# Three changes to an audio tower on one core: who subtracts attention's low parts, fp32 products in the mixture, and where attention's buffers begin

## The reference, cut to what matters

```
h = conv tower(x)
h = h + attention(norm(h))      # 32 query heads, 8 key/value heads, rope, head size 128
h = h + mixture(norm(h))        # top-1 of 8 experts, rank 16
h = h + delay average(norm(h))  # autocorrelation, top 6 lags
h = h + routed linear(norm(h))  # 1024 x 1024 and 8 low-rank experts
```

```
q, k, v = x @ Wq.T, x @ Wk.T, x @ Wv.T          # Wq 4096 x 1024, Wk and Wv 1024 x 1024
out = softmax(rope(q) rope(k).T / sqrt(128)) v  # 4 query heads per key/value head
attention = out @ Wo.T                          # Wo 1024 x 4096

logits = x @ route_w.T                          # 8 experts
weight = one_hot(argmax(logits)) * max(logits)
mixture = (weight * (x @ A.T)) @ Bw.T           # A: 8 x 16 rows, Bw: 8 x 16 columns
```

## Time and profile before

| | us |
|---|---|
| median of 3 runs | 3120.15 (3115.19 to 3120.90) |
| the profiled execution's own time | 3115.31 |
| its span, first to last instruction | 3113.6 |
| attention, from its first projection to its last add | 311.15 to 2513.6 |
| mixture, to its last add | 2513.6 to 2636.6 |

### The profile page before, as it was taken

How to read it: one execution, slowest core, us unless ns; L and a number is a source line. 1 busy time by engine, 2 the same in 40 slices (tenths; PEclk the granted TensorE clock), 3 DMA queues, 4 the chain that set the end, 5 groups by cost and what they waited for, 6 DMA issues and landing times. The chain is left out here.

```text
span 3113.6 us, 37983 instructions
## 1 busy us (share of the span) xinstructions
PE 2854.7 (92%) x13353; PEld 2308.7 (74%) x13353; DVE 1594.4 (51%) x2914; ACT 982.6 (32%) x2029; POOL 915.5 (29%) x394
## 2 busy tenths in 40 slices
PE   8993999999899999989999998999999878749999
PEld 6762777777777777777777777777777667538888
DVE  4886544455544445555444455544445457563222
ACT  3553323333332223333222333232233223531111
POOL 2110433344333334433333442333334100241010
PEclk9995999999999999999999999999999978879999
DMA  5320322223222222322222232222223111010000
GB/s 114 69 54 9 102 75 74 74 88 93 63 75 75 74 74 88 91 65 76 75 74 74 81 93 63 82 75 74 74 71 91 34 55 41 1 61 28 28 27 28
DMA packets 55613, 207.20 MB, mean 67 GB/s; under 512 B 6928, under 2 KB 7312, under 8 KB 53456
## 3 DMA queue, kind: packets, MB, share of 16 engines
q1 hardware_dynamic: 55504, 205.79, 22.2%
HBM read 197.37 MB, written 8.39 MB: 66 GB/s over the span
## 5 line engine op out<-in xcount | busy, mean ns | idle before, releaser
L728 POOL TENSOR_TENSOR at_wlo<-at_wstage,at_whi 128x1024 fp32r<-128x1024 f32 x192 | 477.7, 2488 | 1437.0 <-ACT at_whi L751 1437.0
L993 PE MATMUL at_proj<-qr_xhi,at_whi 128*128 128x512 f32 x1536 | 635.1, 413 | 53.4 <-POOL at_wlo L728 49.0
L995 PE MATMUL at_proj<-qr_xhi,at_wlo 128*128 128x512 f32 x1536 | 609.3, 397 | 0.0
L994 PE MATMUL at_proj<-qr_xlo,at_whi 128*128 128x512 f32 x1536 | 608.8, 396 | 0.0
L993 PEld LDWEIGHTS at_proj<-qr_xhi,at_whi 128*128 128x128 f32 x1536 | 290.2, 189 | 131.2 <-issue 52.7
L994 PEld LDWEIGHTS at_proj<-qr_xlo,at_whi 128*128 128x128 f32 x1536 | 290.3, 189 | 69.9 <-issue 7.5
L995 PEld LDWEIGHTS at_proj<-qr_xhi,at_wlo 128*128 128x128 f32 x1536 | 289.5, 188 | 70.5
L1041 PE MATMUL at_out<-at_wohi,at_ohi 128*128 128x512 f32 x1008 | 314.3, 393 | 8.2 <-DVE at_wolo L720 6.2
L720 POOL TENSOR_TENSOR at_wolo<-at_ostage,at_wohi 128x1024 fp32r<-128x1024 f32 x126 | 312.0, 2497 | 32.7 <-ACT at_wohi L757 32.7
L1041 PE MATMUL at_out<-at_wolo,at_ohi 128*128 128x512 f32 x1008 | 312.5, 391 | 0.0
L1041 PE MATMUL at_out<-at_wohi,at_olo 128*128 128x512 f32 x1008 | 312.5, 391 | 0.0
(11 more groups left out here) (253 smaller groups left out, 4537.1 us busy)
## 6 DMA issues: line engine op xcount, KB each, us to landing
at_wstage<-in_w_qkv_dram SPq DMA_DIRECT2D x192, 512.0 KB, 3.6
at_ostage<-in_w_o_dram SPq DMA_DIRECT2D x128, 512.0 KB, 3.8
cv_x<-in_x_dram SPq DMA_DIRECT2D x32, 512.0 KB, 6.6
out_dram<-h SPq DMA_DIRECT2D x16, 512.0 KB, 2.7
fn_w_lo_raw<-in_w_t_dram SPq DMA_DIRECT2D x8, 512.0 KB, 6.6
fn_qka_lo_raw<-in_qka_t_dram SPq DMA_DIRECT2D x5, 512.0 KB, 5.4
sc_fhi_raw<-in_dft_fwd_dram SPq DMA_DIRECT2D x4, 512.0 KB, 7.1
sc_chi_raw<-in_lag_cos_dram SPq DMA_DIRECT2D x2, 512.0 KB, 9.5
```

Source lines behind the costliest of these rows:

```text
L728: pool.tensor_tensor(w_lo[j % 2][:, :], w_stage.buffers[j % 2][:, :], w_hi[j % 2][:, :].bitcast(F32), ALU.subtract).then_inc(wlo_done, 1)
L993: pe.matmul(proj[:, j % 2, :], hi[:, w], x_hi[:, k, :], start=(k == 0), stop=False)
L994: pe.matmul(proj[:, j % 2, :], hi[:, w], x_lo[:, k, :], start=False, stop=False)
L995: last = pe.matmul(proj[:, j % 2, :], lo[:, w], x_hi[:, k, :], start=False, stop=(k == KT - 1))
```

## The change

1. The low parts of attention's weights and of Wo are subtracted on DVE (`low_w`, `low_o`), at fixed places of DVE's order; POOL is empty in the stage. All four Wo tiles of the last head step go the same way, and `wolo_dve` is gone. ACT rounds w2 before `pT_out` of batch 0 and `soft` of batch 1.
2. Two unused buffers are declared around `x_hi` and `x_lo`: 32 bytes before them and 96 bytes behind. `qr_xhi` and `qr_xlo` begin at byte 288 of 512, and everything of the stage that was at 160 is at 288 too. The convolution's buffers move on by 128 bytes; those of later stages stay.
3. The mixture keeps `ar`, `b`, its rows and `wt` in plain fp32: no high and low parts, 8 fp32 matmuls of 136 columns and 2 of 128x512 a tile in place of 24 and 6. `wt` has two buffers. PE projects tile t before it turns the rows of t+1, and no longer waits for `b` at the start.

```diff
         self.h, self.ident = h, ident
+
+        sb("line_before", [P, 8])
         self.x_hi, self.x_lo = (sb(n, [P, KT, QT], F32R) for n in ("xhi", "xlo"))
+        sb("line_after", [P, 24])
...
-                            if nxt:
+                            if ahead == 0 or nxt:
                                 after(sp, wolo_done, s * HEADS + what[1] + 1)
-                            elif what[1] == 0:
-                                after(sp, wolo_done, s * HEADS + 1)
-                            elif what[1] == 1:
-                                sp.wait_ge(wolo_dve, 1)
-                            if ahead == 0 or nxt:
                                 load_o(s + ahead, g + ahead, r)
...
                     elif att:
                         soft(n, 0)
-                        split(("w", 1, 1), ("o", 0), ("o", 1))
+                        split(("w", 1, 1), ("o", 0), ("o", 1), ("w", 1, 2))
                         pT_out(n)
                         soft(n + 1, 1)
...
-                    split(("w", 1, 2), ("o", 2))
+                    split(("o", 2),)
...
+                def low_w(s, j):
+                    after(dve, whi_done, tile_at(s, j) + 1)
+                    dve.tensor_tensor(w_lo[j % 2][:, :], w_stage.buffers[j % 2][:, :], w_hi[j % 2][:, :].bitcast(F32),
+                                      ALU.subtract).then_inc(wlo_done, 1)
+
+                def low_o(s, r):
+                    after(dve, wohi_done, s * HEADS + r + 1)
+                    dve.tensor_tensor(wo_lo[:, r, :], o_stage[r % 2][:, :], wo_hi[:, r, :].bitcast(F32),
+                                      ALU.subtract).then_inc(wolo_done, 1)
...
                     if nxt:
+                        low_w(s + 1, 1)
+                    if att:
+                        low_o(s, 0)
+                        low_o(s, 1)
+                    if nxt:
                         rope_out(s + 1, 1 - par, 0)
+                    if att and not turn:
+                        top_of(n + 1, 1)
+                    if nxt:
+                        low_w(s + 1, 2)
                     if att:
                         if not turn:
-                            top_of(n + 1, 1)
-                            if not nxt:
-                                low_o(dve, s, 1, wolo_dve)
                             normalize(n + 1)
                         top_of(n + 2, 2)
                         o_split(n)
+                        low_o(s, 2)
+                        low_o(s, 3)
                         normalize(n + 2)
                     if nxt:
+                        low_w(s + 1, 3)
                         rope_out(s + 1, 1 - par, 2)
...
+                    if nxt:
+                        low_w(s + 1, 4)
...
+                    if nxt:
+                        low_w(s + 1, 5)
...
+                    if nxt > 1:
+                        low_w(s + 2, 0)
                     if nxt:
                         rope_out(s + 1, 1 - par, 5)
...
-                steps(dve, lambda: None, step)
+                steps(dve, lambda: low_w(0, 0), step)
```

And in the mixture:

```diff
-        ar = Weight(nc, ctx, "mx_ar", a_route).add_high(nc, ctx)
-        b = Weight(nc, ctx, "mx_b", bw).add_high(nc, ctx)
+        ar = sb("mx_ar", [P, KT * ROUTED])
+        b = sb("mx_b", [P, L])
...
                     after(act, wt_mm, t + 1)
-                    after(act, out_mm, t)
-                    act.copy(wt_hi[:, :], wt[:, 0:P]).then_inc(wthi_done, 1)
+                    if not early(t, 2):
+                        after(act, out_mm, t - 1)
+                    act.copy(wt_sb[i % 2][:, :], wt[:, 0:P]).then_inc(wt_done, 1)
...
                     for c in range(2):
-                        w = slice(c * BANK, (c + 1) * BANK)
-                        pe.matmul(out[:, c, :], wt_hi[:, :], b.hi[:, w], start=True, stop=False)
-                        pe.matmul(out[:, c, :], wt_hi[:, :], b.lo[:, w], start=False, stop=False)
-                        mm = pe.matmul(out[:, c, :], wt_lo[:, :], b.hi[:, w], start=False, stop=True)
+                        mm = pe.matmul(out[:, c, :], wt_sb[par][:, :], b[:, c * BANK:(c + 1) * BANK],
+                                       start=True, stop=True)
...
                 def body(g, i, t, on):
-                    after(pe, rows.lo_done, t + 1)
+                    after(pe, rows.hi_done, t + 1)
+                    after(pe, wh_done, t)
+                    for k in range(KT):
+                        mm = pe.matmul(pj[:, 0:ROUTED], rows.x[i % 2][:, k, :], ar[:, k * ROUTED:(k + 1) * ROUTED],
+                                       start=(k == 0), stop=(k == KT - 1))
+                    mm.then_inc(pj_done, 1)
                     if on(1):
                         rows.turn(pe, t + 1)
-
-                    after(pe, wh_done, t)
-                    xh, xl = rows.x_hi[i % 2], rows.x_lo[i % 2]
...
                     if on(-1):
-                        outputs(t - 1)
+                        if early(t, 2):
+                            pe.wait_ge(b_in, 16)
+                        outputs(t - 1, (i + 1) % 2)
```

More of the change, by code:

```diff
@@ L1102, in __init__ @@
         self.xn = sb("xn", [P, L])
-        self.x_hi = [sb(f"xhi{i}", [P, KT, P], F32R) for i in range(2)]
-        self.x_lo = [sb(f"xlo{i}", [P, KT, P], F32R) for i in range(2)]
+        if split:
+            self.x_hi = [sb(f"xhi{i}", [P, KT, P], F32R) for i in range(2)]
+            self.x_lo = [sb(f"xlo{i}", [P, KT, P], F32R) for i in range(2)]
+        else:
+            self.x = [sb(f"x{i}", [P, KT, P]) for i in range(2)]
         self.st = sb("st", [P, GROUP, 2, 6])
@@ L1213, in normalize, with turn, copy @@
                        scale=self.all_rstd[:, bass.ds(t, 1)]).then_inc(self.normed, 1)
+    def turn(self, pe, t):
+        after(pe, self.normed, t + 1)
+        after(pe, self.hi_done, t)
+        for k in range(KT):
+            last = pe.transpose(self.tp[:, k // 4, (k % 4) * P:(k % 4 + 1) * P],
+                                self.xn[:, k * P:(k + 1) * P], self.ident[:, :])
+        last.then_inc(self.turned, 1)
+    def copy(self, act, t, par, used, count):
+        after(act, self.turned, t + 1)
+        after(act, used, count)
+        act.copy(self.x[par][:, :, :], self.tp[:, :, :].rearrange("p a (k t) -> p (a k) t", t=P))\
+           .then_inc(self.hi_done, 1)
 class Weight:
@@ L1342, in mixture_stage @@
         wh = sb("mx_wh", [P, ER])
-        wt_hi = sb("mx_wthi", [P, P], F32R)
-        wt_lo = sb("mx_wtlo", [P, P], F32R)
+        wt_sb = [sb(f"mx_wt{i}", [P, P]) for i in range(2)]
         pj = ctx.enter_context(nc.psum_tensor("mx_pj", [P, BANK], F32))
@@ L1357, in _ @@
             def _(sp):
-                ar.load(sp)
+                sp.dma_start(ar[:, :], a_route).then_inc(ar_in, 16)
                 sp.dma_start(numbers[:, :], experts).then_inc(numbers_in, 16)
-                b.load(sp)
+                sp.dma_start(b[:, :], bw).then_inc(b_in, 16)
                 tables.load(sp)
@@ L1369, in before @@
                 def before():
-                    ar.high(act)
                     rows.normalize(act, 0, 0)
-                    rows.high(act, 0, 0, pj_done, 0)
+                    rows.copy(act, 0, 0, pj_done, 0)
                     rows.normalize(act, 0, 1)
-                    b.high(act)
                 def body(g, i, t, on):
                     if on(1):
-                        rows.high(act, t + 1, (i + 1) % 2, pj_done, t)
+                        rows.copy(act, t + 1, (i + 1) % 2, pj_done, t)
                     if on(2):
@@ L1388, in before @@
                 def before():
-                    ar.low(dve)
-                    rows.low(dve, 0, 0)
-                    b.low(dve)
                     dve.wait_ge(numbers_in, 16)
@@ L1418, in body @@
                 def body(g, i, t, on):
-                    if on(1):
-                        rows.low(dve, t + 1, (i + 1) % 2)
                     route_of(t)
@@ L1454, in body @@
                     if on(1):
                         rows.turn(pe, t + 1)
-                    after(pe, wh_done, t)
-                    xh, xl = rows.x_hi[i % 2], rows.x_lo[i % 2]
-                    for k in range(KT):
-                        w = slice(k * ROUTED, (k + 1) * ROUTED)
-                        pe.matmul(pj[:, 0:ROUTED], xh[:, k, :], ar.hi[:, w], start=(k == 0), stop=False)
-                        pe.matmul(pj[:, 0:ROUTED], xh[:, k, :], ar.lo[:, w], start=False, stop=False)
-                        mm = pe.matmul(pj[:, 0:ROUTED], xl[:, k, :], ar.hi[:, w], start=False, stop=(k == KT - 1))
@@ L1464, in body @@
[L1464 removed]
                     if on(-1):
[L1466 removed]
+                        if early(t, 2):
+                            pe.wait_ge(b_in, 16)
+                        outputs(t - 1, (i + 1) % 2)
                     after(pe, wh_done, t + 1)
[L1468 removed]
+                    after(pe, wt_done, t)
                     pe.transpose(wt[:, 0:P], wh[:, :], ident[:, :]).then_inc(wt_mm, 1)
[L1470 removed]
```

(1 more changed line is left out.)

53 lines of the change are left out of this document (11 added, 42 removed).

## The result

| | before | after |
|---|---|---|
| median, us | 3119.72 | 3009.60 (3005.65 to 3012.60) |
| the profiled execution's own time | 3115.31 | 3012.60 |
| its span | 3113.6 | 3010.9 |

A forecast was written before the change was run, and what follows sets the result against it. It took PE's list to bound attention, 2202.45 of 3113.6 us. Stall -47, last step -1, pace -27 and mixture -18 sum to -93 from the profiled 3115.3, so 3022; median put at 3023, range 3007 to 3053.

The forecast's parts named there:

- The stall before tile 2: Attention's 28 regular head steps: PE no longer waits for POOL's low part of w2, -47 us, bounds 0 and 49.
- The last step: Attention's last head step: PE's 6.19 us wait for DVE shortens by about one subtraction, -1 us.
- The turn steps: Attention's three turn steps wait for the next quarter's rows rather than for POOL: 0.
- The pace: Attention's projections: matmuls with both operands at byte 288 start 0.2267 us apart, not 0.2333; -27 us, bounds 0 and 30.
- rival A: Operand positions change nothing; the pace comes from what matmuls follow or which buffers they read: 3050 us, chance 0.12.
- Outputs: Attention's output matmuls keep equal bytes and their 0.227 us pace: 0.
- The mixture: The mixture stage in plain fp32, with an earlier start and shorter tiles: -18 us, bounds -8 and -26.
- the start: The mixture's start: tile 0's `wt` comes 8 to 11 us earlier, taken as 10.
- a tile bound by PE's list: Middle tiles of the mixture: 4.75 us instead of 5.49, 0.74 less in each of some 11, 8 in all.
- the tiles at the clock's lower level: Mixture tiles in which the clock is at its lower level: no gain counted.
- Rivals B and D: B: another attention wait replaces the stall, middle 3046, chance 0.10. D: DVE bounds each head step, 3191, chance 0.03.
- Rival C: The mixture gains its start alone, or less, its tiles held by DVE's routing chain: 3032 us, chance 0.08.

The follow-up runs named there:

- e9: The changed kernel, but POOL subtracts all low parts as before, with ACT's new order kept: 3018.0 us, ratio 0.9681 to the kernel before.
- e10: The changed kernel with DVE subtracting, but ACT rounds w2 behind the softmax of batch 1 as before: 3046.8 us, ratio 0.9775 to the kernel before.
- e1: The changed kernel without its two unused buffers, rows at byte 256 and weights at 160 again: 3033.5 us, ratio 0.9735 to the kernel before.
- e5: The changed kernel without the unused buffer in front, so rows and weights both begin at byte 256: 3006.0 us, one run.
- e7: The changed kernel with other unused-buffer sizes, rows at byte 288 and weights at 416: 3030.6 us, one run.
- e6: The changed kernel with other unused-buffer sizes, rows at byte 160 and weights at 256: 3036.1 us, one run.
- e8: The changed kernel with other unused-buffer sizes, rows at byte 288 and weights at 320: 3027.8 us, one run.
- e3: The changed kernel with the mixture as before (split products, weights rounded first): 3038.1 us, ratio 0.9745 to the kernel before; mixture 124.3 us.
- e11: The changed kernel with two more 1.22 us subtractions on DVE ahead of Wo's low part 2 in each head step: 3051.6 us, one run.

## Why the prediction was right, point by point

**The stall before tile 2** (-47): right. The wait is gone in all 28 regular steps, and is worth 1.74 us each at the old pace, 49. The laying out of DVE's order held: low_w(2) was put 2.7 us ahead of PE, and is 1150.35 - 1147.85 = 2.5; Wo's low parts were put 1.2 ahead of the outputs and are 1155.93 - 1154.70 = 1.23. What the working blurred is the reason: it names ACT's order and DVE's speed in one breath; e9 and e10 give 39 to 44 of 54 us to the order. It also set the 1.65 us of the 128x4 operation against 0.69 of a 128x512 one; the same operation takes 0.17 without POOL.

**The last step** (-1): the wait fell from 6.19 to 4.25 us, the step by 1.8.

**The turn steps** (0): 80.25, 80.37 and 81.04 us before, 81.71, 82.10 and 82.11 after, 4.3 in all the other way. Over all kernels here they took 78.1 to 83.0, one kernel's three among themselves as much as 4.2 apart (e1: 78.76, 82.97, 81.21). PE stands several times in them, and their length follows how long the clock is at its lower level: 6.8 us of each of the three before, 13.7, 13.7 and 10.2 after, none of e5's second (78.14) and 13.7 of its first (81.71). The window of the first has a clock of 0.96 before and 0.92 after. So these 4.3 us are most likely chance: the profiled run was the slowest of four.

**The pace** (-27): right in mechanism, and rival A is out. By the ratios it is 27 us; that this is the number forecast is in part luck, since it is not all where it was counted. Projections gained 233.6 - 228.3 = 5.3 ns in the mean over 4608, 24 us, instead of 6.6 over 21 of 24 matmuls: the first ten after a change of work stay slow also with equal bytes. Outputs, counted at 0, gained 1.5 ns over 3072, 5 us: their operands were at equal bytes all along, but a projection with unequal ones hands a lag on to the first matmuls of the output behind it (1.3 ns in the mean in e7 too, 0.1 and 0.2 in e6 and e8). In a regular step it is 0.87 us, 24 in 28 steps.

**The mixture** (-18): the term that was mis-sized, by 14. Its terms, from the distances between the `wt` transposes:
- the start, 10 forecast: 23.55 us from attention's last matmul to tile 0's `wt`, now 12.65: 10.9.
- a tile bound by PE's list, 0.74 less in 11: 0.83 to 0.93 less in eight of twelve, 0.5 to 1.5 in the others, 11.2 in all. 4.56 us is just the list, 16 x 0.116 + 4 x 0.43 + 9 x 0.109; the waits of 0.1 to 0.2 that the forecast left are not there.
- the tiles at the clock's lower level, "I count nothing": tile 0 to 1 went from 9.53 to 5.70, 4 to 5 from 9.19 to 4.62, 5 to 6 from 6.20 to 4.56: 10.0 less. This is the step of the prediction that failed: it put the tiles at the lower level at nothing, and gave no reason. In the kernel before the lower level (1.2 GHz) lay over two windows of the stage; in the changed one over its first 11 us:

```profile
2520.78:2545.10 24.32, 18.25 (x79) 17.20 (x80) 9.03 (x26) 7.65 (x8) 5.96 (x6) 0.50 0.30 115
2545.10:2565.60 20.50, 16.83 (x124) 14.70 (x123) 18.43 (x63) 7.63 (x10) 0.00 (x0) 1.00 0.00 1
2565.60:2575.90 10.30, 10.30 (x46) 9.61 (x44) 4.56 (x14) 2.42 (x3) 0.00 (x0) 0.50 0.01 2
```
```profile
2441.70:2453.00 11.30, 7.95 (x33) 7.05 (x33) 1.71 (x10) 3.66 (x4) 0.00 (x0) 0.55 0.83 297
2453.00:2531.70 78.70, 70.18 (x432) 53.00 (x431) 53.60 (x205) 33.79 (x45) 5.97 (x6) 1.00 0.03 12
```
The first group is of before, the second of after. e3 shows the two windows of before again, 77 us earlier in the run: they belong to the split mixture and not to when it begins. Which property of it, its longer pauses or its kind of matmul, is open. At tile 4, where both kernels stand 3.1 to 3.3 us for DVE's routing, the clock can fall again. Of ten profiles with this mixture three (the changed kernel's, e5 and e7) keep the clock there and take 4.62 us from tile 4 to 5; the other seven take 6.2 to 6.3. So 1.6 us of this term are luck. On the other side tile 0 to 1 took 5.70 in five of them and 4.87 in five, and the whole stage 90.9 to 93.4.

**Rivals B and D**: no wait took the stall's place; 1.218 us a low part, where 1.4 would have used up the margin and e11 shows what happens then. Rival C is out as well: the tiles gained as much as the start.

**The median.** The sum of -93 was taken from the profiled run, 4.8 below the median before, and only 1 us was added; by the medians the same sum gives 3027. Against the 110 measured by the medians the sum is 17 short: 14 are the mixture's.

## What to carry to other kernels

Read PE's pace from the distances between starts, and compare two stretches with the same shapes: here a constant 3% between them was where the operands begin, and two unused buffers of 128 bytes in all removed it. When an engine waits for a slow helper, ask first when the helper's input was issued: moving one rounding forward gave 44 us, and 39 with the faster helper in place; halving the helper's time gave 15 alone and 10 behind the move. Where a stage has stretches at the lower clock, forecast it as a range with and without them; a change that shortens the pauses can take those stretches away with it, though which property did so here is open.

## What the hardware showed that was not expected

- Matmuls of 128x512 in fp32r whose two operands begin at the same byte of 512 settle at 226.7 ns from start to start. At offsets of 32, 96 and 128 bytes to each other they take 233 to 234, in e6 to e8 as in e1. At equal bytes the byte itself (160, 256, 288) doesn't matter.
- A projection, which follows work of another kind, takes some ten matmuls until the 226.7 is reached, and outputs behind it have it from the first; with unequal bytes a projection never reaches it.
- DVE's 128x4 operation takes 0.17 us, and 1.64 in the median when POOL subtracts beside it (57 of 128 in e9); its 128x1024 subtraction takes 1.22 beside PE and ACT at work.
